# A ring of eight tanh blocks, and one tanh instruction over two neighbouring blocks

## The reference, cut to what matters

```
n    = layernorm(x)
feat = n @ W                         # per token
txt  = text @ Ws + b                 # per text token
rho[f, t] = sum_d w[d] * tanh(txt[t, d] + feat[f, d])
att  = softmax(rho + mask)           # over the 77 text tokens
x    = x + tanh(g0) * (tanh(att.text.Wcw + ..) * n + tanh(att.text.Wcb + ..))
p    = softmax(layernorm(x) @ router.T); top 2 of 8
x    = x + tanh(g1) * sum over the two experts of p * (gelu(n2 @ w1.T) @ w2.T)
```

## Time and profile before

| | |
|---|---|
| times of three runs | 596.78, 591.98, 596.64 us; median 596.64 |
| span of the profiled execution | 591.3 us |
| TensorE busy (matmul) | 523.8 us, 89% of the span |
| VectorE busy | 359.5 us, 61% |
| ScalarE busy | 354.4 us, 60% |
| GpSimd busy | 119.2 us, 20% |
| chain that ended last | TensorE 57%, VectorE 19%, ScalarE 9%, DMA 5% |

### The profile page before, as it was taken

The page is one execution under the profiler, slowest core; times in us unless marked ns, Lnnn a source line. Parts: engine busy times, 40 slices in busy tenths (PEclk is TensorE's granted clock), DMA queues, the critical chain, the costliest instruction groups (busy, mean ns, idle before and its releaser), DMA issues.

```text
span 591.3 us, 10151 instructions
## 1 busy us (share of the span) xinstructions
PE 523.8 (89%) x3408; PEld 336.8 (57%) x3409; DVE 359.5 (61%) x1190; ACT 354.4 (60%) x314; POOL 119.2 (20%) x96
## 2 busy tenths in 40 slices
PE   3897869775799898989899999999899999999994
PEld 2432323101355453445454555788799999999993
DVE  4799998898875799895799987376111111111110
ACT  1499999987998988999978999141011111111110
POOL 2000000050001253501243111136222222222222
PEclk9888979667889979999979999999899999999998
DMA  4011940046213027433127433348756666656541
GB/s 132 1 37 60 422 169 0 1 156 208 98 54 116 10 66 185 167 91 90 71 52 238 137 114 97 130 133 256 228 175 185 180 185 180 178 178 178 170 99 18
DMA packets 32922, 77.56 MB, mean 131 GB/s; under 512 B 4560, under 2 KB 25680, under 8 KB 26736
## 3 DMA queue, kind: packets, MB, share of 16 engines
q1 hardware_dynamic: 25536, 67.31, 33.7%
q0 software_dynamic: 7344, 9.72, 8.8%
HBM read 60.73 MB, written 16.29 MB: 130 GB/s over the span
## 4 chain that ended last, share of the span: by engine, by line
PE 57%; DVE 19%; ACT 9%; DMA 5%; SPq 4%; issue 3%; POOL 1%; POOLq 0%; DVEq 0%
PE h_ps L696 19%; PE y_bank L708 18%; PE rho L661 12%; DVE hbuf L860 8%; ACT hbuf L554 8%; PE misc L641 3%; DMA out<-x_res 2%; SPq L370 1%; PE xsT_bank L684 1%; SPq L371 1%; PE misc L633 1%; DMA w_st<-in_w 1%; PE xsT_bank L650 1%; ACT hbuf L560 1%; DVE rows L838 1%
## 5 line engine op out<-in xcount | busy, mean ns | idle before, releaser
L554 ACT ACTIVATE hbuf<-hbuf 128x2048 f32<-128x2048 f32 (+2 forms) x160 | 247.3, 1594 | 40.3 <-DVE hbuf L860 40.0
L860 DVE TENSOR_SCALAR hbuf<-featT,txtb 128x512 f32<-128x512 f32 x525 | 216.3, 480 | 21.6 <-PE rho L661 20.5
L661 PE MATMUL rho<-hbuf,wpad 128*32 128x512 f32 x1232 | 177.0, 660 | 32.1 <-ACT hbuf L554 17.1
L696 PEld LDWEIGHTS h_ps<-xsT,w_st 128*128 128x128 f32 x1280 | 151.2, 194 | 27.3 <-issue 24.4
L696 PE MATMUL h_ps<-xsT,w_st 128*128 128x128 f32 x1280 | 157.4, 280 | 1.5 <-issue 1.2
L708 PE MATMUL y_bank<-w_sb,hgT 128*128 x640 | 153.2, 390 | 2.3 <-DVE y_sb L1035 2.3
L708 PEld LDWEIGHTS y_bank<-w_sb,hgT 128*128 128x128 f32 x640 | 119.6, 193 | 38.8 <-issue 24.1
L583 ACT ACTIVATE hgT<-h_ps 128x1024 f32<-128x1024 f32 x40 | 40.8, 1020 | 166.6 <-PE h_ps L696 166.5
L511 POOL DMA_INDIRECT out<-y_sb,meta x40 | 69.0, 1726 | 300.5 <-DMA out<-y_sb,meta 130.0
L661 PEld LDWEIGHTS rho<-hbuf,wpad 128*32 128x32 f32 x1232 | 31.0, 114 | 119.4 <-ACT hbuf L560 41.9
L1021 DVE COPY xsT<-xsT_bank 128x256 f32<-128x256 f32 x40 | 17.0, 424 | 86.5 <-PE xsT_bank L684 86.5
(11 more groups left out here) (134 smaller groups left out, 185.7 us busy)
## 6 DMA issues: line engine op xcount, KB each, us to landing
w_st<-in_w SPq DMA_DIRECT2D x40, 1024.0 KB, 5.0
w_sb<-in_w SPq DMA_DIRECT2D x8, 1024.0 KB, 12.4
xs<-row_scratch SPq DMA_DIRECT2D x40, 132.5 KB, 4.5
row_scratch<-pad SPq DMA_DIRECT2D x33, 132.5 KB, 19.3
hgT<-in_x SPq DMA_DIRECT2D x4, 512.0 KB, 3.6
x_res<-in_x SPq DMA_DIRECT2D x4, 512.0 KB, 4.8
out<-x_res SPq DMA_DIRECT2D x4, 512.0 KB
out<-y_sb,meta POOLq DMA_INDIRECT x40, 6.2
```

The source lines that it names most:

```text
L554: ins = s.activation(h, h, ACT.Tanh)
L661: ins = t.matmul(rho[q % 2][32 * j:32 * j + 32, :], wpad[:, c, 31 - r:63 - r], hbuf[:, k % HB, j, :], start=(k == 0), stop=(last and c == ...
L696: ins = t.matmul(h_ps[:, k * P:(k + 1) * P], w1_st[:, par, c, k * P:(k + 1) * P], xsT[:, c, :], start=(c == 0), stop=(c == DC - 1))
L860: ins = v.tensor_scalar(hbuf[:, k % HB, j:j + 1, :], featT[:, c, q:q + 1, :], txtb[:, c, bb, CG * r + j:CG * r + j + 1], None, ALU.add)
```

## The change

The ring gets eight slots. A pair is two neighbouring blocks k and k + 1, from block 4 on in quarter 0 and from block 14 on in the others, up to block 37; ScalarE waits until both are summed and takes the tanh of all summed columns of both with one instruction, then the direct columns of the second, if it has any, then raises `h_ok` once for the pair, and then does the gelu of either block. TensorE waits for the count of groups instead of blocks, so it reads both blocks after that. A quarter has 17 pairs (quarter 0) or 12 (the others): 53 in all. In quarter 0 the direct column moves from every third block to the second block of every pair (19 instead of 13 direct columns, so that the first block of a pair is summed whole).

```diff
@@ -35,7 +35,7 @@
 RS = -(-T // CG)
 TP = RS * CG
 NBLK = RS * DC
-HB = 4
+HB = 8
 NEG = 1e30
 FILL = -3e38
 EPS = 1e-5
@@ -320,14 +320,30 @@
                     DVE_TILE.setdefault(g, []).append((name, i))
         assert [sum(g < LAST for g in at) for at in (UP, TURN, DOWN, GELU, XOUT, YOUT)] == [14, 14, 12, 13, 14, 11]

-        DIRECT0 = range(0, NBLK, 3)
+        PAIRED_FROM = (4, 14, 14, 14)

         def summed(q, k):

             n = CG if k // DC < RS - 1 else T - CG * (RS - 1)
+            if n < CG:
+                return n, n
             if q == 0:
-                return n, n - (1 if n == CG and k in DIRECT0 else 0)
+                return n, n - k % 2
             return n, n - (3 if k < 6 else 1 if k < 14 else 0)
+
+        def tanh_groups(q):
+
+            k = 0
+            while k < NBLK:
+                n = 2 if k >= PAIRED_FROM[q] and summed(q, k + 1)[0] == CG else 1
+                yield k, n
+                k += n
+
+        groups_of = [list(tanh_groups(q)) for q in range(NQ)]
+
+        def groups_until(q, k):
+
+            return sum(len(g) for g in groups_of[:q]) + sum(first <= k for first, _ in groups_of[q])

         QUADS = (NT - 1 - (SURE + 1)) // 4
         LOOP_END = SURE + 1 + 4 * QUADS
@@ -544,26 +560,29 @@
             act.wait_ge(consts_in, 16 * N_CONST)
             s.activation(tg[:], gs[:, 0:2], ACT.Tanh).then_inc(gate_t, 1)

-            def tanh_block(q, k, bb):
-                act.wait_ge(sum_ok, NBLK * q + k + 1)
-                n, m = summed(q, k)
-                r, c = k // DC, k % DC
+            def tanh_group(q, k, blocks, bb):
+
+                last = k + blocks - 1
+                act.wait_ge(sum_ok, NBLK * q + last + 1)
+                n, m = summed(q, last)
+                whole = CG * (blocks - 1)
                 at = 0
-                if m:
-                    h = hbuf[:, k % HB, 0:m, :]
+                if whole + m:
+                    h = hbuf[:, k % HB:k % HB + blocks].rearrange("p b j s -> p (b j) s")[:, 0:whole + m, :]
                     ins = s.activation(h, h, ACT.Tanh)
                     if m == n:
                         ins.then_inc(h_ok, 1)
-                    if (k, at) in ACT_S[q]:
-                        settle(ACT_S[q][k, at], q - 1)
+                    if (last, at) in ACT_S[q]:
+                        settle(ACT_S[q][last, at], q - 1)
+                r, c = last // DC, last % DC
                 for j in range(m, n):
-                    ins = s.activation(hbuf[:, k % HB, j, :], featT[:, c, q, :],
+                    ins = s.activation(hbuf[:, last % HB, j, :], featT[:, c, q, :],
                                        ACT.Tanh, bias=txtb[:, c, bb, CG * r + j:CG * r + j + 1])
                     at += 1
                     if j == n - 1:
                         ins.then_inc(h_ok, 1)
-                    if (k, at) in ACT_S[q]:
-                        settle(ACT_S[q][k, at], q - 1)
+                    if (last, at) in ACT_S[q]:
+                        settle(ACT_S[q][last, at], q - 1)

             def settle(step, q):
                 if step == "exp":
@@ -583,11 +602,11 @@
                 s.activation(hgT[:, par].rearrange("p c k -> p (c k)"), h_ps[:], ACT.Gelu).then_inc(hg_ok, 1)

             for q in range(NQ):
-                for k in range(NBLK):
-                    tanh_block(q, k, q // 2)
-                    if NBLK * q + k in ACT_TILE:
-                        i = ACT_TILE[NBLK * q + k]
-                        gelu(i, i % 2)
+                for k, blocks in groups_of[q]:
+                    tanh_group(q, k, blocks, q // 2)
+                    for g in range(NBLK * q + k, NBLK * q + k + blocks):
+                        if g in ACT_TILE:
+                            gelu(ACT_TILE[g], ACT_TILE[g] % 2)
             gelu(13, 1)
             settle("exp", NQ - 1)
             settle("tanh", NQ - 1)
@@ -654,7 +673,7 @@
             def rho_block(q, k):

                 r, c = k // DC, k % DC
-                pe.wait_ge(h_ok, NBLK * q + k + 1)
+                pe.wait_ge(h_ok, groups_until(q, k))
                 n = CG if r < RS - 1 else T - CG * (RS - 1)
                 for j in range(n):
                     last = r == RS - 1 or (r == RS - 2 and j >= T - CG * (RS - 1))
```

## The result

The changed kernel took 622.32 us in the median of four runs (618.80 to 624.59), the kernel before 594.47 in the four runs beside it: a ratio of 1.0465, interval 1.0427 to 1.0503. Forecast were 610, 597 to 619: the direction was right and the time lies above the range. The profiled execution has a span of 621.9 us and took 623.63, so some 2 us lie around the span.

The account below looks back on a forecast made before the run. ScalarE, with VectorE, was taken to bound quarter 0, ScalarE or TensorE the later halves. Quarter 0's -3.9 and waits of +3.4, +7.9, +7.0 on 591.3 gave 605.7; 4 more made 610 us, range 597 to 619.

Parts of the forecast that it names:

- the longer round trip: Quarters 1 to 3, transpose to tanh of the copy's block: 7.4 us if first of its pair, against 4.1 single.
- The sum above takes none of it: Half clock behind TensorE's new waits, three of 3.5 us and more and three of 2, was put at nothing.
- the entries: First pair of a second half: TensorE waits 2.15 us more in quarters 2 and 3; quarter 1's hides behind a load.
- The rival on the clock: TensorE's clock falls in the new waits: 5.5 us for three, 10.9 for six; about 7 added gives 617; chance 0.2.
- The row that spoke for it: TensorE row at 160.65 before the change: after a 3.07 us wait, two blocks took 3.74 us instead of 1.92.
- The waits: TensorE waiting for pairs adds 3.4 us in quarter 1, 7.9 in quarter 2 and 7.0 in quarter 3.
- Quarter 0: ScalarE runs pairs at 3.67 us, VectorE stays ahead; scores_out comes at about 98.7 instead of 102.58: -3.9 us.
- the tail and the first 14 blocks shift whole: Expert tiles of about 200 us and first 14 blocks of quarters 1 to 3 are only shifted, not changed.
- the tanh of a pair of 3.5 us: ScalarE's 4096-column tanh: 3.48 us taken, with bounds of 3.36 and 3.60.
- no cost of the three late gelus: Gelus inside pairs (114, 142, 156) come 1.8 us later, covered by 3.8 us of TensorE work: nothing, or 1 us.
- the ring can't buy the waits back in quarters 1 to 3: In-order VectorE stops at every x_out four blocks ahead of TensorE, whatever the ring's depth.
- The 4 us added for what lies around the span: Runs shown lay 0.7 to 5.5 us above the span; 4 added to 605.7 gave 610 us.

Follow-up runs that it names:

- the waits filled: Changed kernel plus 25 matmuls that nobody reads, ahead of rho of nine blocks where TensorE waits for a pair: 613.35 us, ratio 1.0314 to the kernel before.
- the tenth experiment: Changed kernel with VectorE's copies at their early place and pairs only from block 16 on in quarters 1 to 3: 617.75 us, ratio 1.0389 to the kernel before.

## Why the prediction was wrong

The forecast's mechanism was right: a pair comes late by the longer round trip past VectorE's copy, and TensorE waits in the places that were named. What the sum then made of it fell short: it gave a span of 605.7 us where 621.9 were measured. Of these 16.2 us the clock has some 9.6, the waits themselves 3.6 and quarter 0 2.9.

**The step that failed** is the one sentence "The sum above takes none of it", on the clock, with the reason that "the entries' slow blocks lie partly inside the next wait". That reason holds for the entries alone, and for less than half of their price. In quarter 3 the first pair's 3.71 us wait was followed by rho of 3.54, 1.6 more than at full clock. Rho of block 136 came 43.8 us after `scores_out` in before (at 326.32), 47.7 after it (347.84), and 46.7 with the waits filled (340.79): the next wait, the 0.57 that shows when the clock is full, hides some 0.6, and 1.0 is paid. The other four long waits (108, 114, 142, 156) pay 1.6 each (3.36 instead of 1.99 behind 2.16 us, and what follows). So behind six new waits of quarters 2 and 3 the clock cost 8.5 us that the sum put at nothing: the change's two quarters less those of the filled waits, 4.2 and 4.3. In quarter 1 filling gives the change 3.5 and single blocks 2.4 (90.3 less 87.9), so some 1.1 is new there, an estimate. The medians of the change and of the filled waits lie 9.0 apart, their three quarters 12.0 in the profiles; their quarter 0 differs by 1.8 the other way without an edit there, so I can't narrow it further. The rival on the clock, with a price of 1.8 for each of six waits (10.9), was right in kind and near in size; I gave it 0.2 and took 7. The row that spoke for it, 3.74 after a wait of 3.07, should have been put into the sum as a price for every wait of that length, and the 1.00 of the earlier trace rows not taken as evidence against it, since the stretches that had it had no such wait.

By the Trainium skill ("TensorE: Matmul & The Clock Gate", HAM oscillation), waits that recur in a loop put the clock down in each round. The trace of the changed kernel agrees, with slow work behind all six; that of the tenth experiment agrees in part, as two of its waits of 2.16 and 2.17 us have full speed behind them.

**The waits** were forecast at 3.4 + 7.9 + 7.0 = 18.3 us. With full clock they are 4.4 + 8.9 + 8.6 = 21.9, of which the 4.4 is an estimate from two kernels' profiles. Each wait ahead of 102, 114, 142, 150 and 156 came 0.1 to 0.2 above its forecast, the entry of quarter 3 at 2.9 instead of 2.15, and in quarter 1 the forecast has none of the wait of 2.31 us ahead of blocks 58 and 59:

```profile
150.72 3.23 PE L680 MATMUL rho<-hbuf,wpad 128*32 128x512 f32 x16 [2.31 <-ACT hbuf L572]
```

**Quarter 0** was the second miss: -3.9 forecast, -1.0 measured. I stepped ScalarE through the pairs and took TensorE as covered. ScalarE's pitch came out (3.7 a pair), though after the first pair it waited 1.4 us for sums where 0.6 were forecast. But TensorE's projections stand behind blocks that the pairs hold, and in this execution one of them, behind a wait of 1.77, took 3.50 in place of 1.98, as TensorE's timeline of the changed kernel has it:

```profile
85.02 1.06 PE L680 MATMUL rho<-hbuf,wpad 128*32 128x512 f32 x8 [1.77 <-ACT hbuf L579]
86.02 3.50 PE L660 MATMUL misc<-hgT,W_sb 128*128 128x512 f32 x4
```

From there TensorE works without a wait to the end of the quarter: it, and not ScalarE, set the end. Of the 3.5 us that the ring gave in its own profile, the pairs took back 2.5.

Right were: the tail and the first 14 blocks shift whole (215.4 against 215.5 for the rest; rho of block 133 comes 35.6 us after `scores_out` in both); the tanh of a pair of 3.5 us; no cost of the three late gelus in the places looked at, as TensorE's waits there end with a tanh; and that the ring can't buy the waits back in quarters 1 to 3. The 4 us added for what lies around the span, where 2 do, hid 2 us of the miss by luck.

## What to carry to other kernels

Merging two units of work into one instruction saves a tenth of a microsecond here and holds the first unit back by a whole one. No kernel with pairs beat the ring alone. Before merging, look for every in-order stop that lies within a unit of the merged pair, and move the stop behind the pair first (21 of 28 us). The deeper ring helped in quarter 0, where VectorE waited 6.1 us for free slots and meets no copy, and gave nothing in quarters 2 and 3, where it stops at the copies. A new wait of TensorE is to be priced with a stretch at half clock behind it, from a row of the same kernel; that price is the likely one, not a certain one.

## What was not expected of the hardware

Waits as short as 2.16 us had work at half clock behind them (3.36 instead of 1.99 us in the changed kernel), but the same wait doesn't have it every time. After 2.17 and 2.16 us the tenth experiment's `down` took 1.99. After 1.77 us the projection took 3.50 in the changed kernel and 1.98 with pairs in quarter 0 only. Even 3.80 us had full speed behind it once, ahead of blocks 134 and 135 with the ring of four:

```profile
358.97 1.92 PE L680 MATMUL rho<-hbuf,wpad 128*32 128x512 f32 x16 [3.80 <-ACT hbuf L572]
360.83 1.99 PE L727 MATMUL y_bank<-w_sb,hgT 128*128 x8
```

So the work behind a wait does not take the same time in every execution; what decides it, no run here shows.
